# Two softmax attentions: scores by groups of 32 rows, norms by four tiles, and a new order of the engines' queues

## What is computed

```python
q = (query @ Wq.T + bq).reshape(bsz, tgt_len, NUM_HEADS, HEAD_DIM).transpose(0, 2, 1, 3)
k = (key @ Wk.T + bk).reshape(bsz, src_len, NUM_HEADS, HEAD_DIM).transpose(0, 2, 1, 3)
v = (value @ Wv.T + bv).reshape(bsz, src_len, NUM_HEADS, HEAD_DIM).transpose(0, 2, 1, 3)
scores = jnp.einsum('bhtd,bhsd->bhts', q, k) * scale
scores = jnp.where(causal_mask[None, None], neg_inf, scores)
scores = jnp.where(key_padding_mask[:, None, None, :], neg_inf, scores)
attn = jax.nn.softmax(scores, axis=-1)
out = jnp.einsum('bhts,bhsd->bhtd', attn, v)
```

## Time and profile before

| what | value |
|---|---|
| median of three runs | 3278.0 us |
| profiled execution, its own time | 3283.84 us |
| span of its trace | 3282.1 us |
| masked attention, first start to last `final` | 237 to 566 us |
| unmasked attention, the same | 1016 to 1330 us |
| busy share of the span | PE 90%, DVE 85%, ACT 71%, POOL 71% |

### The profile page before, as it was taken

One profiled execution on the slowest core, in us unless ns is written; L12 is line 12 of the kernel. 1 busy time (PEld: TensorE's weight loads), 2 busy tenths in 40 slices (PEclk: granted clock), 3 DMA queues, 4 the chain that ended last, 5 costly groups with the idle time before them and its releaser, 6 DMA issues.

```text
span 3282.1 us, 78570 instructions
## 1 busy us (share of the span) xinstructions
PE 2945.8 (90%) x24633; PEld 2215.6 (68%) x24646; DVE 2780.9 (85%) x9101; ACT 2342.4 (71%) x7540; POOL 2319.9 (71%) x3111
## 2 busy tenths in 40 slices
PE   6639998289667999599999999999999999999998
PEld 5526775167435777477777777777777777777776
DVE  4369997599898998698898989898999889898987
ACT  3275665878796666477777777777777777777776
POOL 1179997565687666377777777777777777777777
PEclk7559998589678999799999999999999999999999
DMA  3000000022000110300000000000000000000000
GB/s 107 19 10 17 16 17 8 17 74 72 5 1 17 29 31 28 114 21 8 7 9 9 7 8 8 9 8 8 7 9 9 8 7 9 9 8 8 8 8 5
DMA packets 133086, 63.73 MB, mean 19 GB/s; under 512 B 20544, under 2 KB 132288, under 8 KB 132672
## 3 DMA queue, kind: packets, MB, share of 16 engines
q1 hardware_dynamic: 132672, 58.70, 6.3%
HBM read 41.82 MB, written 8.45 MB: 15 GB/s over the span
## 4 chain that ended last, share of the span: by engine, by line
PE 57%; ACT 1%; DVE 1%; POOL 0%; DMA 0%; issue 0%; SPq 0%; POOLq 0%; ACTq 0%; DVEq 0%
PE ps_sw_a L2173 23%; PE ps_sw_d L2173 21%; PE ps_sw_w L2219 4%; PE ps_sw_w L2206 3%; PE ps_sw_s L2188 2%; PE ps_sw_s L2230 2%; PE ps_sw_m L2195 1%; ACT sw_scaled L1914 0%; PE ps_sw_m L2181 0%; DVE sw_v_part L2069 0%; DMA sw_v<-in_L_ffn_v_w 0%; ACT sw_probs L1963 0%; DVE sw_v_low L2008 0%; ACT sw_v_high L1969 0%; PE ps_sw_w L2236 0%
## 5 line engine op out<-in xcount | busy, mean ns | idle before, releaser
L1914 ACT ACTIVATE sw_scaled<-ps_sw_a,sw_gate_o 128x128 f32<-128x128 f32 x2048 | 620.3, 447 | 254.1 <-PE ps_sw_a L2173 248.2
L1914 ACT ACTIVATE sw_scaled<-ps_sw_a,sw_gate_v 128x128 f32<-128x128 f32 x2048 | 597.4, 448 | 194.4 <-PE ps_sw_a L2173 192.7
L2069 DVE SCALAR_TENSOR_TENSOR sw_o_part<-ps_sw_d,sw_gate_o,sw_o_part 128x128 f32<-128x128 f32 x1920 | 554.9, 338 | 63.2 <-PE ps_sw_d L2173 60.5
L1841 POOL TENSOR_TENSOR sw_v_pair<-sw_v_part,sw_scaled 128x256 f32<-128x256 f32 x512 | 382.1, 746 | 156.0 <-DVE sw_v_part L2069 98.9
L2069 DVE SCALAR_TENSOR_TENSOR sw_v_part<-ps_sw_d,sw_gate_v,sw_scaled 128x128 f32<-128x128 f32 x1024 | 303.7, 337 | 122.1 <-PE ps_sw_d L2173 104.7
L1867 POOL TENSOR_TENSOR sw_o_rest<-sw_o_rest,sw_scaled 128x256 f32<-128x256 f32 x384 | 285.4, 743 | 157.9 <-ACT sw_scaled L1914 120.8
L2069 DVE SCALAR_TENSOR_TENSOR sw_v_part<-ps_sw_d,sw_gate_v,sw_v_part 128x128 f32<-128x128 f32 x1024 | 304.1, 337 | 0.0
L1870 POOL TENSOR_TENSOR sw_o_rest<-sw_o_rest,sw_scaled 128x256 f32<-128x256 f32 x384 | 282.6, 736 | 30.1
L1846 POOL TENSOR_TENSOR sw_v<-sw_v_pair 128x128 f32<-128x128 f32 x512 | 243.8, 476 | 40.1
L985 POOL TENSOR_TENSOR at_key_wide<-at_keyT,c_half_heads 128x1024 f32<-128x1024 f32 x128 | 242.6, 1895 | 4.2 <-ACT at_keyT L1082 4.2
L2173 PE MATMUL ps_sw_a<-sw_v_high,sw_xT_high 128*128 128x512 f32 x512 | 234.6, 458 | 8.2 <-DVE sw_v_low L2008 8.2
(11 more groups left out here) (337 smaller groups left out, 8584.4 us busy)
## 6 DMA issues: line engine op xcount, KB each, us to landing
at_ctxT<-ctx_T SPq DMA_DIRECT2D x128, 64.0 KB, 1.8
re_values<-in_ctx SPq DMA_DIRECT2D x128, 64.0 KB, 2.4
x<-in_x SPq DMA_DIRECT2D x16, 256.0 KB, 3.4
l_ctx<-in_ctx SPq DMA_DIRECT2D x16, 256.0 KB, 3.0
re_ctx<-in_ctx SPq DMA_DIRECT2D x16, 256.0 KB, 3.2
scratch_x<-x SPq DMA_DIRECT2D x64, 64.0 KB, 1.9
sw_x<-scratch_x SPq DMA_DIRECT2D x64, 64.0 KB, 1.9
sw_x_res<-scratch_x SPq DMA_DIRECT2D x64, 64.0 KB, 1.8
```

Of the source, the lines that this page charges most:

```text
L1841: pool.tensor_tensor(v_pair[:, h % 2], v_part[:, h], scaled[:, h % 4, 2:4], ALU.add)\
L1914: act.activation(scaled[:, h % 4, e], ps_a[h % 2][:, e], ACT.Copy, scale=gates[:, s, h, HALF_E + e:HALF_E + e + 1]).then_inc(a_scaled[kind ...
L2069: dve.scalar_tensor_tensor(out=acc[:, e % 2], in0=ps_d[h % 2][:, e], scalar=gates[:, s, h, e:e + 1], in1=before, op0=ALU.mult, op1=ALU.add ...
```

## The change

- Scores: eight matmuls of 32 contracted rows and 256 columns instead of four of 64 and 512, each group of 32 rows into a PSUM bank of its own (four banks). The widened keys are half as wide (`quarter_heads`).
- PSUM: the turned probabilities have one bank instead of two and are turned and copied in two halves; q, k and v share a bank; the output moves from the bank of the weighed values to that of the turned rows.
- Norms: stats and aggregate per tile, variance, power and negated mean for four tiles at once, and xhat on ScalarE.
- Masks: built for 16 tiles at once; the wait for the padding transfer moves into the first of these.
- Order: the peak ahead of the residual, heads divided ahead of the values, all lags of the main pipe larger by five. `turn_heads` keeps its wait for `keep_x`. Masked `centre` stays on GpSimd.
- The context is read where it lies instead of being copied tile by tile by DMA.

```diff
--- before.py
+++ after.py
...
+    quarter_heads = (p[:, None] % 32 // HD == np.arange(HEADS // 4)[None]).astype(np.float32)
...
-    NS = 4
+    N, NS, ROWS, QUARTER = GROUP, 4, 32, HEADS // 4
...
-        ctxT = k.sb(name + "_ctxT", [P, NS, P])
...
-        key_wide = k.sb(name + "_key_wide", [P, NS, HALF, P])
+        key_wide = k.sb(name + "_key_wide", [P, NS, QUARTER, P])
...
-        ps_s = k.psum(name + "_scores", [P, HEADS, S])
-        ps_t = k.psum(name + "_turned", [P, HALF, P])
-        ps_a = k.psum(name + "_a", [P, 2, P])
-        ps_qk = k.psum(name + "_qk", [P, 2, P])
-        ps_v = k.psum(name + "_v", [P, P])
+        ps_s = k.psum(name + "_scores", [P, 4, 512])[:, :, 0:QUARTER * S].rearrange("p r (j s) -> p r j s", j=QUARTER)
+        ps_t = k.psum(name + "_turned", [P, HALF // 2, P])
+        ps_a = k.psum(name + "_a", [P, 3, P])
+        ps_qkv = k.psum(name + "_qkv", [P, 3, P])
+        ps_v = ps_qkv[:, 2]
         ps_o = k.psum(name + "_o", [P, 512])
         pv = ps_o[:, 0:HEADS * (HD + 1)].rearrange("p (h d) -> p h d", h=HEADS)
-        out_ps = ps_o[:, 256:256 + D]
-        q = k.sems(name, *LN_SEMS, "consts", "ctx_read", "x_turned", "xT", "proj", "qT", "keyT", "key", "val", "ones",
...
-                straight([(0, fetch)] + ([(10, store)] if out is not None else []), NS)
...
+                def rstd(g, s):
+                    pool.wait_ge(q["var_eps"], g + 1)
+                    if g >= 4:
+                        pool.wait_ge(q["xhat"], N * (g - 3))
+                    pool.tensor_tensor(small["rstd"][:, s], small["var"][:, s], C["minus_half"][:].broadcast_to([P, N]),
+                                       ALU.pow).then_inc(q["rstd"], 1)
...
+                stages = [(10, centre)] if masked else []
+                straight(stages + [(7, add_bias), (1, by_group(rstd)), (8, widen)], NS)
...
+                def build_mask(i, s, r):
+                    if i % CHUNK == 0:
+                        if i == 0:
+                            dve.wait_ge(q["consts"], 48)
+                        dve.scalar_tensor_tensor(out=mask[:, i:i + CHUNK], in0=padding[:, i:i + CHUNK], scalar=NEG,
+                                                 in1=causal[:].unsqueeze(1).broadcast_to([P, CHUNK, S]),
+                                                 op0=ALU.mult, op1=ALU.min).then_inc(q["mask"], 1)
 
...
+                    dve.wait_ge(q["h_kept"], last(i + 2))
...
+                def negated_mean(g, s):
+                    dve.wait_ge(q["rstd"], g + 1)
+                    if g >= 4:
+                        dve.wait_ge(q["xhat"], N * (g - 3))
+                    dve.scalar_tensor_tensor(out=small["nmr"][:, s], in0=mv[:, s, :, 0], scalar=-1.0, in1=small["rstd"][:, s],
+                                             op0=ALU.mult, op1=ALU.mult).then_inc(q["nmr"], 1)
+
+                def moments(i, s, r):
+                    dve.bn_stats(stats[:, i % (2 * N)], X[:, i]).then_inc(q["stats"], 1)
+
+                def aggregate(i, s, r):
+                    dve.wait_ge(q["stats"], i + 1)
+                    dve.bn_aggr(mv[:, i // N % 4, i % N], stats[:, i % (2 * N)]).then_inc(q["moments"], 1)
+
+                def variance(g, s):
+                    dve.wait_ge(q["moments"], N * g + N)
+                    dve.tensor_scalar(small["var"][:, s], mv[:, s, :, 1], EPS, None, ALU.add).then_inc(q["var_eps"], 1)
+                stages = [(10, read_scores), (10, centre), (14, final), (2, by_group(negated_mean)), (0, moments),
+                          (1, aggregate), (1, by_group(variance)), (12, normalise), (8, place_values)]
+                straight(([(7, build_mask)] if masked else []) + stages, NS)
...
+                def norm(i, s, r):
+                    act.wait_ge(q["nmr"], i // N + 1)
+                    if i >= NS:
+                        act.wait_ge(q["x_turned"], i - NS + 1)
+                    g = i // N % 4
+                    act.activation(xhat[:, s], X[:, i], ACT.Identity, bias=small["nmr"][:, g, i % N:i % N + 1],
+                                   scale=small["rstd"][:, g, i % N:i % N + 1]).then_inc(q["xhat"], 1)
...
+                def keep_probs(part):
+                    def step(i, s, r):
+                        act.wait_ge(q["p_turned"], 2 * i + part + 1)
+                        if i >= NS:
+                            act.wait_ge(q["pv"], i - NS + 1)
+                        act.activation(probs_T[:, s, part * HALF // 2:(part + 1) * HALF // 2], ps_t, ACT.Copy)\
+                            .then_inc(q["p_kept"], 1)
+                    return step
...
-                straight([(8, keep_heads), (3, keep_q), (6, keep_probs), (2, keep_x), (5, exp)], NS)
+                straight([(13, keep_heads), (8, keep_q), (11, keep_probs(0)), (6, norm), (11, keep_probs(1)), (7, keep_x),
+                          (10, exp)], NS)
...
-                    pe.wait_ge(q["heads"], last(i + 2))
-                    if isinstance(i, int) and i == TILES - 1:
+                    if i:
                         pe.wait_ge(q["x"], i)
...
+                def turn_probs(part):
+                    def step(i, s, r):
+                        pe.wait_ge(q["exp"], i + 1)
+                        if 2 * i + part:
+                            pe.wait_ge(q["p_kept"], 2 * i + part)
+                        for n in range(HALF // 2):
+                            j = part * HALF // 2 + n
+                            m = pe.transpose(ps_t[:, n], probs[:, s, 2 * j:2 * j + 2].rearrange("p h k -> p (h k)"),
+                                             C["ident"][:])
+                        m.then_inc(q["p_turned"], 1)
+                    return step
...
+                    pe.wait_ge(q["key"], i + 1)
+                    pe.wait_ge(q["qT"], i + 1)
+                    if i:
+                        pe.wait_ge(q["masked" if masked else "centred"], i)
+                    for b in range(2):
+                        t = slice(b * S, (b + 1) * S)
+                        for quarter in range(4):
+                            h = slice(quarter * ROWS, (quarter + 1) * ROWS)
+                            m = pe.matmul(ps_s[t, quarter], qT[h, s, t], key_wide[h, s, :, t], start=True, stop=True)
                     m.then_inc(q["scores"], 1)
 
...
+                    pe.matmul(ps_qkv[:, 1], W["k"][:], CT[:, i], start=True, stop=True)
...
-                straight([(8, turn_heads), (9, output), (3, project), (6, turn_probs), (7, weigh), (2, turn_x),
-                               (4, scores)], NS)
...
+                straight([(13, turn_heads), (14, output), (8, project), (11, turn_probs(0)), (12, weigh), (11, turn_probs(1)),
+                          (7, turn_x), (9, scores)], NS)
...
```

More of the change, by code:

```diff
@@ L149, in build_constants @@
     nc = k.nc
[L150 removed]
+    for name, shape in (("ident", [P, P]), ("half_heads", [P, HEADS // 2]),
+                        ("quarter_heads", [P, HEADS // 4]), ("half_mask", [P, 2])):
         C[name] = k.sb("c_" + name, shape)
@@ L907, in softmax_attention @@
     masked = layer == 1
-    NS = 4
+    N, NS, ROWS, QUARTER = GROUP, 4, 32, HEADS // 4
     HALF = HEADS // 2
-    last = lambda v: min(v, TILES) if isinstance(v, int) else v
+    CHUNK = 16
+    last = lambda v: min(v, TILES)
     with k.scope():
-        L = ln_buffers(k, name, NS)
-        ctxT = k.sb(name + "_ctxT", [P, NS, P])
+        stats = k.sb(name + "_stats", [P, 2 * N, 6])
+        mv = k.sb(name + "_mv", [P, 4, N, 2])
+        small = {n: k.sb(f"{name}_{n}", [P, 4, N]) for n in ("var", "rstd", "nmr")}
+        xhat = k.sb(name + "_xhat", [P, NS, D])
         xT = k.sb(name + "_xT", [P, NS, P])
@@ L1007, in normalise @@
                     dve.wait_ge(q["rsum"], i + 1)
-                    if not first(i, NS):
+                    if i >= NS:
                         dve.wait_ge(q["h_turned"], i - NS + 1)
@@ L1144, in project @@
                     pe.wait_ge(q["xT"], i + 1)
-                    pe.wait_ge(ctx_in[s], 16 * r + 16)
-                    if not first(i, 1):
+                    if i:
                         pe.wait_ge(q["qT"], i)
```

141 lines of the change are left out of this document (59 added, 82 removed).

## The result

The changed kernel takes 3291.4 us (median of 20 runs), the one before 3280.5 (20 runs): the ratio is 1.0036, 95% interval 1.0028 to 1.0044. It is slower by 0.36%. The forecast was +1.6 us, with a range that holds this time; the result lies some 9 us above the forecast, and of the three outcomes "faster" had been given the highest chance.

The account below looks back on a forecast made before the run. GpSimd (masked, 4.65 us a tile) and TensorE (unmasked, 4.66) were taken as the bounds. Masked +11.7 and unmasked -10.1 gave net +1.6 on 3278.0, about 3279 us; range 3255 to 3297.

Parts of the forecast that it names:

- masked, first to last turn_heads: Masked attention's full tiles: -10.5 us from shorter periods, +23.2 from held VectorE operations in 14 groups, +3 from masks.
- masked filling: Start of masked attention: padding wait moves to the first mask, hiding 5 of 7.46 us; longer pipe costs 2; net -3.
- unmasked, first to last turn_heads: Unmasked attention's full tiles: 60 periods shorter by 0.185 us each, -11.1 us.
- unmasked filling: Start of unmasked attention: five more pipe iterations holding only stats and the group's power, about +2 us.
- the loop over keep_x: TensorE to ScalarE and back: turn_heads waits for keep_x behind the second probabilities copy, setting a period of 4.475 us.
- The hold: Masked attention: GpSimd's centre holds VectorE's variance and negated mean, making two iterations in four last 5.01 and 5.60 us.
- A smaller hold (1): Masked attention: negated mean escapes centre or variance waits only partly; 3264, 3272 or, without both, 3256 us; chance 0.24.
- No loop (2): Both attentions: the wait through keep_x is not closed, so TensorE's 4.29 us rules; near 3262 us; chance 0.06.
- VectorE not getting in between two operations of GpSimd (3): Masked attention: held instructions also wait for the bias operation behind centre, 12 us more, 3291 us; chance 0.14.
- Only four places (4): Scores on TensorE: only four passes run at once, so 4.66 us stays; 3295 us; chance 0.08.
- VectorE as the bound: VectorE's work per tile in the attentions was put at about 3.7 us, under the 4.475 period, so not limiting.
- Three masks: Masked attention: three 16-tile mask operations outside the filling, each delaying VectorE's iteration about 1 us, +3 in all.

Follow-up runs that it names:

- e1: Changed kernel with x turned and kept ahead of the second half of the probabilities and its copy: 3276.1 us, 0.9990 of the kernel before.
- e2: Changed kernel with VectorE's negated mean issued ahead of the final sum, 0.2 us earlier: 3281.1 us, 0.9993 of the kernel before.
- e10: Changed kernel with variance and negated mean each as four 128x1 operations instead of one 128x4, same order: 3281.4 us, 1.0002 of the kernel before.
- e3: Changed kernel with negated mean and variance both ahead of the final sum, each an iteration later: 3278.4 us, 0.9992 of the kernel before.
- e11: Changed kernel with variance and negated mean as four 128x1 operations each, and x turned and kept first: 3249.3 us, 0.9906 of the kernel before.
- e5: Changed kernel with x turned and kept first, and variance and negated mean ahead of the final sum only when masked: 3251.2 us, 0.9910 of the kernel before.
- e4: Changed kernel with variance and negated mean ahead of the final sum in both attentions, x turned and kept first: 3260.8 us, 0.9935 of the kernel before.

## Why the prediction was right and wrong

| term | forecast | measured |
|---|---|---|
| masked, first to last turn_heads | -10.5 + 23.2 + 3 = +15.7 | 306.7 - 294.9 = +11.8 |
| masked filling | -3 | -0.1 |
| masked end | -1 | +0.4 |
| unmasked, first to last turn_heads | -11.1 | 284.4 - 288.1 = -3.7 |
| unmasked filling | +2 | +2.9 |
| unmasked end | -1 | -0.3 |
| sum | +1.6 | +10.9 |

Filling is from the border to the first turn_heads, end from the last turn_heads to the next border.

**The mis-sized term** is the length of the loop over keep_x: "with some 0.05 for the signal the next turn_heads starts at 4.475". Counted from turn_heads, the turning of the probabilities, the weighing, the second half and its copy began at 1.36, 1.95, 2.99 and 3.68 instead of 1.32, 1.91, 2.96 and 3.65; keep_x ended at 4.45 instead of 4.42; turn_heads began 0.14 behind it instead of 0.05. The period came to 4.59. No row stood behind the 0.05. The mechanism was right (e1 removes it and finds 4.31 below), its size off by 0.115 x 60 = 7 us, which is most of the 9.3 missed. Such a sum stands against a period only 0.185 longer, so 0.1 takes more than half of the gain.

**The hold** was forecast in place, kind and height: negated mean 1.885 (1.9 to 2.0), variance 1.494 (near 1.5), iterations 4.92 and 5.47 (5.01 and 5.60), two long ones in four, TensorE waiting for heads. That the negated mean starts 0.04 behind centre, where 0.03 was forecast, is a narrow margin. e2 and e10 show the hold as the cause: the same values from a 0.2 us earlier place, or from another form at the same place, cost 0.15 or 0.56. Against the short iterations a group costs 1.13 (10.39 - 2 x 4.63), not 1.66; this and the loop, by which the short ones last 4.63 and not 4.475, nearly cancel. There are 13 such groups and not 14, and the period before was 4.68 and not 4.65: the 43 operations by which 200 us were divided are not all whole inside the window. So that the masked attention as a whole came out at +12.0, where +11.7 was forecast, is luck in part.

**The masked filling** gained nothing in all, but the step that was forecast did happen. The first masked read comes 14.80 us behind the attention's start instead of 18.14, 3.3 earlier (about 3 was forecast); the changed kernel first, then the one before:

```profile
245.67 1.23 DVE L1043 TENSOR_TENSOR at_raw<-ps_at_scores,at_mask 128x1024 f32<-128x1024 f32 x1 [0.38 <-PE ps_at_scores L1194]
```

```profile
255.36 1.23 DVE L1022 TENSOR_TENSOR at_raw<-ps_at_scores,at_mask 128x1024 f32<-128x1024 f32 x1 [0.99 <-PE ps_at_scores L1139]
```

It is not all of the 7.46 us, for the mask waits for the padding in place of the first stats, and the second tile's values stand behind the mask on VectorE, so that TensorE's second projection waits:

```profile
239.79 1.22 DVE L1017 SCALAR_TENSOR_TENSOR at_mask<-at_padding,at_causal 128x1024 f32<-128x1024 uint8 x1 [5.16 <-DMA at_padding<-in_mask_BxS_bf]
...
241.68 0.42 DVE L1066 TENSOR_TENSOR at_val_wide<-ps_at_qkv,c_half_mask 128x256 f32<-128x256 f32 x1
...
242.25 0.76 PE L1203 MATMUL ps_at_qkv<-at_xT,w_q 128*128 128x128 f32 x2 [4.41 <-DVE at_val_wide L1066]
```

The 3.3 us are lost again before the first turn_heads. There are five more iterations, and TensorE works at 1.2 GHz for longer: its clock rises 34.8 us behind the attention's start, before the change 17.7 behind it. The stretch from 10 to 35 us behind the start, changed kernel first (columns as above):

```profile
240.87:265.87 25.00, 22.24 (x193) 15.24 (x193) 17.18 (x34) 11.15 (x27) 15.01 (x15) 0.50 0.00 1
```

```profile
247.22:272.22 25.00, 19.78 (x199) 12.52 (x198) 21.61 (x47) 10.82 (x25) 21.78 (x23) 0.85 0.06 17
```

The prediction had no term for the clock. What the later rise costs, no run isolates: in e3, whose clock rose 27.1 us behind the start, filling and first period are 3.0 us shorter than in the changed kernel.

**The rivals.** A smaller hold (1): no, both held. No loop (2): no, but e1 shows what it would have given, 17 us in the unmasked attention alone. VectorE not getting in between two operations of GpSimd (3): no; stats starts at 405.49 beside the bias operation at 405.50. Its time, 3291, is the time measured, by chance: the number alone would have spoken for a mechanism that the trace refutes. Only four places (4): no, 0.69 for 16 passes. VectorE as the bound (some 3.7 a tile): not even at the periods of 4.31 and 4.37 in e11. Three masks: 1.7 us each, about 0.3 on each period, less than the 1 forecast; where the period is 4.37 (e5) they cost 1 each.

## What to carry to other kernels

When a step is taken off the engine that bounds, list the waits that were met with room to spare, with their room. keep_x had 0.63; the shorter scores took 0.37 of it, the copy ahead of keep_x 0.42 (keep_x ended at 4.45 instead of 4.03) and the signal to turn_heads 0.14, which makes some 0.3 a tile of waiting. The repair is to issue the short reader that frees a bank ahead of the long copy. Small vector operations beside a busy GpSimd are to be placed, or put in a form that is not held, with each attention or stage looked at by itself (e4 against e5). Compare stages by their borders as well as whole times: here the untouched rest moved by up to 9 us between profiles, as much as the effect. Read the granted clock of a stage's filling and end before a few us there are put down to an edit.

## What the runs showed of the hardware

- The hold of VectorE by GpSimd depends on the form (durations in us). Held to the end of GpSimd's two-input operation: 128x4 from two tensors (1.885 and 0.63), 128x1 from two tensors (0.99), 128x4 from one (1.494). Not held: 128x1 from one tensor with a constant (0.15, four in 0.34) or with a scalar per partition (four in 0.56). The Trainium skill, "SBUF — State Buffer", section "SBUF: two separate sides", has a VectorE operation with two SBUF inputs, or in a mode that uses two ports, and a GpSimd one that reads SBUF shut each other out for the whole instruction. The rows of the two-tensor forms agree. For the forms with one tensor it depends by that rule on whether they run in such a mode, which no trace here shows: 128x4 was held and 128x1 was not. e10 changes the form and the number of elements at once; one tensor of four adjacent elements was not tried. The hold also depends on GpSimd's operation: in the gated feed-forward of the kernel before, the one-tensor 128x4 took 0.30 inside a GpSimd operation with one input of 1.92 (857.30 to 859.22), so there it was not held to the end, whatever the rule would have.
- It works the other way too: in e4 a bias operation of GpSimd took 1.43 us instead of 0.45 when it came behind the mask's start:

```profile
381.17 1.79 DVE L1017 SCALAR_TENSOR_TENSOR at_mask<-at_padding,at_causal 128x1024 f32<-128x1024 uint8 x1
...
381.83 1.43 POOL L988 TENSOR_TENSOR x<-x,w_bias 128x128 f32<-128x128 f32 x1
```

- The filling runs at TensorE's lower clock, and for how long varies from execution to execution. The stretch from 23 to 31 us behind the start of the unmasked attention, of e5 (first fence) and e1 (second), whose code there is the same (us; busy time of the five engines PE, PEld, DVE, ACT, POOL with counts; granted clock; DMA share, GB/s):

```profile
1016.29:1024.29 8.00, 8.00 (x80) 5.87 (x80) 4.65 (x12) 4.13 (x11) 2.86 (x4) 0.51 0.00 0
```

```profile
1049.42:1057.42 8.00, 8.00 (x136) 6.12 (x136) 6.51 (x16) 6.71 (x16) 3.90 (x5) 0.97 0.00 0
```

In the 23 us before, both have 123 matmul records, a granted clock of 0.50 and TensorE busy for 16.7 us. In e1 the clock rises to 2.4 GHz 23.5 us behind the start and in e5 30.8 behind it, 7.3 us later after the same work. e5's attention is 5.0 us longer (303.4 against 298.5): 3.2 of it lie in the filling and first period, and 1.9 in the last two periods and the end, where e5's clock fell 9.8 us before the end and e1's 2.0. The five more iterations of the pipe lie in this filling.
